# Feeding the next batch's first scan rows early, fc2 in four other banks, and identity matmuls between the tiles of layer norms

## The reference

```python
# block 0: bidirectional state-space block and gated MLP, both with adaptive layer norm
h, gate = adaln(x, c, ...)                      # LN(x) * (1 + scale) + shift
x = x + gate * (ssm(h, fwd) + flip(ssm(flip(h), bwd)))
h, gate = adaln(x, c, ...)
x = x + gate * ((silu(h @ w1) * (h @ w2)) @ w3)
# ssm: xs, z = split(h @ in_w); xs = silu(xs); dt, B, C from xs @ xproj_w
#      state[d, s] = state[d, s] * exp(dt_t * A[d, s]) + dt_t * x_t * B_t[s];  y_t = sum_s state * C_t[s]
#      y = (y + xs * Dskip) * silu(z) @ out_w          (512 channels, 64 states)
# block 1: attention with 16 heads of 16, unit-length q and k, then FFN
x1 = ln(x) * (scale1 + 1) + shift1
x = x + (softmax(unit(q) * sm @ unit(k).T) @ v @ proj_w.T + proj_b) * gamma1
x2 = ln(x) * (scale2 + 1) + shift2
x = x + (gelu(x2 @ fc1_w.T + fc1_b) @ fc2_w.T + fc2_b) * gamma2
```

## Time and profile before

| | |
|---|---|
| median of 3 runs | 3326.49 us |
| profiled execution, its own time | 3327.19 us |
| its span | 3325.4 us |
| granted TensorE clock, mean | 0.989 |
| TensorE busy | 3211.2 us (97%), weight loads 2670.8 us (80%) |
| VectorE busy | 2775.5 us (83%) |
| ScalarE busy | 2801.9 us (84%) |
| GpSimd busy | 2516.3 us (76%) |
| DMA | 187.19 MB, mean 56 GB/s |

### The profile page before, as it was taken

The page is one execution under the profiler, slowest core; times in us unless marked ns, Lnnn a source line. Parts: engine busy times, 40 slices in busy tenths (PEclk is TensorE's granted clock), DMA queues, the critical chain, the costliest instruction groups (busy, mean ns, idle before and its releaser), DMA issues.

```text
span 3325.4 us, 60434 instructions
## 1 busy us (share of the span) xinstructions
PE 3211.2 (97%) x23656; PEld 2670.8 (80%) x23656; DVE 2775.5 (83%) x2969; ACT 2801.9 (84%) x4968; POOL 2516.3 (76%) x1120
## 2 busy tenths in 40 slices
PE   8999999999899999999989999999999999999999
PEld 7989898974698988996468999899637898888854
DVE  3999999966399999996549999999555999999962
ACT  4999999955599999994569999999457999999744
POOL 3999999950299999993039999999305999999800
PEclk9999999999999999999999999999999999999999
DMA  4211212200212111120021121212002222111100
GB/s 164 71 66 52 74 52 72 65 32 1 77 55 66 67 65 63 61 69 22 1 86 58 66 69 56 71 53 71 13 1 86 64 66 65 57 58 58 39 13 7
DMA packets 57900, 187.19 MB, mean 56 GB/s; under 512 B 6664, under 2 KB 12808, under 8 KB 56848
## 3 DMA queue, kind: packets, MB, share of 16 engines
q1 hardware_dynamic: 57616, 183.33, 16.3%
HBM read 180.14 MB, written 3.16 MB: 55 GB/s over the span
## 4 chain that ended last, share of the span: by engine, by line
PE 65%; POOL 17%; ACT 8%; issue 7%; DVE 2%; DMA 1%; SPq 0%; DVEq 0%; ACTq 0%; POOLq 0%
POOL states L567 16%; PE bank L977 16%; PE bank L959 13%; PE bank L960 8%; PE bank L855 7%; ACT decay L710 4%; PE bank L1176 4%; PE bank L1049 3%; ACT inflow_tok L704 3%; PE bank L1095 2%; PE bank L1197 2%; PE bank L1276 2%; PE bank L1209 2%; DVE states L1413 1%; PE bank L1030 1%
## 5 line engine op out<-in xcount | busy, mean ns | idle before, releaser
L567 POOL TENSOR_TENSOR states<-states,c_rows 128x1024 f32<-128x1024 f32 x1020 | 2390.2, 2389 | 440.0 <-DMA c_rows<-c_spill 389.5
L1413 DVE TENSOR_TENSOR_SCAN states<-decay,bank 128x512 f32<-128x512 f32 x2048 | 2357.0, 1204 | 196.7 <-ACT decay L710 147.9
L710 ACT ACTIVATE decay<-dt,a_log 128x512 f32<-128x512 f32 x2048 | 1307.6, 714 | 0.0
L977 PE MATMUL bank<-ident,states 128*128 128x128 f32 x8192 | 1240.9, 274 | 30.2 <-POOL states L567 6.6
L959 PE MATMUL bank<-ident,inflow_tok 128*128 128x128 f32 x6144 | 1034.4, 277 | 31.7 <-DVE states L1413 16.0
L704 ACT ACTIVATE inflow_tok<-dtx_tok,b_tok 128x512 f32<-128x512 f32 x1536 | 995.9, 715 | 42.3 <-PE bank L960 39.1
L977 PEld LDWEIGHTS bank<-ident,states 128*128 128x128 f32 x8192 | 951.8, 141 | 71.3 <-POOL states L567 63.3
L959 PEld LDWEIGHTS bank<-ident,inflow_tok 128*128 128x128 f32 x6144 | 714.2, 141 | 190.9 <-issue 98.4
L960 PE MATMUL bank<-b_diag,dtx_tok 128*128 128x128 f32 x4096 | 792.4, 275 | 0.0
L960 PEld LDWEIGHTS bank<-b_diag,dtx_tok 128*128 128x128 f32 x4096 | 619.0, 191 | 0.0
L705 ACT ACTIVATE b_diag<-ident,b_tok 128x128 f32<-128x128 f32 x512 | 201.1, 393 | 0.0
(11 more groups left out here) (154 smaller groups left out, 1975.0 us busy)
## 6 DMA issues: line engine op xcount, KB each, us to landing
c_rows<-c_spill SPq DMA_DIRECT2D x256, 512.0 KB, 3.7
xproj_w<-in_xproj_w SPq DMA_DIRECT2D x32, 320.0 KB, 4.2
in_w<-in_in_w SPq DMA_DIRECT2D x16, 512.0 KB, 4.8
in_w<-in_fc_w SPq DMA_DIRECT2D x8, 512.0 KB, 5.3
xproj_w<-in_w SPq DMA_DIRECT2D x8, 512.0 KB, 5.1
xproj_w<-in_fc_w SPq DMA_DIRECT2D x4, 1024.0 KB, 4.8
x_ahead<-in_x SPq DMA_DIRECT2D x4, 512.0 KB, 5.2
y_gated<-in_mod_w SPq DMA_DIRECT2D x4, 512.0 KB, 8.3
```

The costliest lines, as they stand in the source:

```text
L567: pool.tensor_tensor(pair, pair, c_row, ALU.mult).then_inc(weighed, 1)
L710: act.activation(decay[:, r % SLOTS * KI + k, :], dt[:, d, k, :], ACT.Exp, scale=a_neg[:, d, k, s:s + 1]).then_inc(decay_ready, 1)
L977: last = pe.matmul(banks[KI + t][:, k * P:(k + 1) * P], states[:, r % SLOTS * KI + k, t * P:(t + 1) * P], ident[:], is_transpose=True, sta ...
L1413: dve.tensor_tensor_scan(states[:, slot, time], decay[:, slot, time], banks[k % INFLOW_BANKS][:, time], 0.0, ALU.mult, ALU.add).then_inc(s ...
```

## The change

- SyncE loads `c_rows` for rows 0 and 2 of the next batch right behind the wait for attention's last turned lanes, ahead of the wait for fc1; the scan's loop leaves those two out from the second batch on.
- fc2 and its residual use banks 4 to 7 (`OUT_BANK`). `add_rows` of tile t waits for gelu t + 1, which frees bank 4 + t; a new wait for all eight gelus stands ahead of fc2's products.
- ScalarE, behind the last gelu, loads the table set of Exp and feeds rows 0 and 1 of the next batch, ahead of fc2's four copies; the loop leaves those two feeds out from the second batch on.
- TensorE's wait for the copies moves from the head of a batch to the first `sum_up`, which is the first to write banks 4 to 7.
- In `ln` (layer norms 1 and 3) TensorE issues `KEEP` = 2 matmuls of the identity with 256 columns of `qkv_w` into bank 4 behind each turned tile. Nobody reads their product.

```diff
+OUT_BANK = 4
+KEEP = 2
@@ SyncE, scan loop
-                    spread_rows(b, r)
+                    if r > HALF or not b:
+                        spread_rows(b, r)
@@ SyncE, behind the scan
                     sp.wait_ge(lanes_turned, (b + 1) * NG)
+                    sp.wait_ge(c_spilled, (b * 2 + 3) * 16)
+                    spread_rows(b + 1, 0)
+                    spread_rows(b + 1, HALF)
                     sp.wait_ge(fc1_mm, (b + 1) * KF)
@@ ScalarE, copy_rows
-                    act.activation(x_of[i + 1][:, t, :], banks[t][:, 0:D], ACT.Copy).then_inc(res_copied, 1)
+                    bank = banks[OUT_BANK + t if i == 3 else t]
+                    act.activation(x_of[i + 1][:, t, :], bank[:, 0:D], ACT.Copy).then_inc(res_copied, 1)
@@ ScalarE, scan loop
-                    feed_scan(b, r)
+                    if r > 1 or not b:
+                        feed_scan(b, r)
@@ ScalarE, behind the gelus
+                if not last:
+                    act.preload_act_table_set("exp_and_others")
+                    feed_scan(b + 1, 0)
+                    feed_scan(b + 1, 1)
                 for t in range(TT):
                     act.wait_ge(res_mm, (b * RES + 3) * TT + t + 1)
                     copy_rows(b, 3, t)
@@ TensorE, ln
                 for t in range(TT):
                     ln_turn(b, i, t)
+                    for _ in range(KEEP):
+                        pe.matmul(banks[O_BANK][:, 0:D], ident[:], qkv_w[:, 0, 0:D], start=True, stop=True)
@@ TensorE, sum_up
+                    if first and not r and b and not t:
+                        pe.wait_ge(res_copied, b * 3 * TT)
@@ TensorE, batch
-                pe.wait_ge(res_copied, b * 3 * TT)
@@ TensorE, behind fc1 (add_rows and residual_tile take a bank offset, at)
                 for t in range(TT):
-                    pe.wait_ge(fc1_ready, b * KF + KH + t + 1)
-                    add_rows(t, x_att, 1)
+                    pe.wait_ge(fc1_ready, b * KF + t + 1)
+                    add_rows(t, x_att, 1, OUT_BANK)
                 pe.wait_ge(fc2_gated, b + 1)
+                pe.wait_ge(fc1_ready, (b + 1) * KF)
                 for t in range(TT):
-                    residual_tile(t, lambda c, t: gelu_h[:, c, t * P:(t + 1) * P], lambda c: fc2_w[:, c, :], KF)
+                    residual_tile(t, lambda c, t: gelu_h[:, c, t * P:(t + 1) * P], lambda c: fc2_w[:, c, :], KF, OUT_BANK)
```

More of the change, by code:

```diff
@@ L1039, in turn_high, with add_rows, residual_tile @@
                 last.then_inc(y_turned, 1)
-            def add_rows(t, x, bias=None):
-                pe.matmul(banks[t][:, 0:D], ident[:], x[:, t, :], start=True, stop=False)
+            def add_rows(t, x, bias=None, at=0):
+                pe.matmul(banks[at + t][:, 0:D], ident[:], x[:, t, :], start=True, stop=False)
                 if bias is not None:
-                    pe.matmul(banks[t][:, 0:D], ident[0:1, 0:1].to_broadcast([1, P]), bias_g[:, bias, :], start=False, stop=False)
-            def residual_tile(t, lhs, rhs, steps):
+                    pe.matmul(banks[at + t][:, 0:D], ident[0:1, 0:1].to_broadcast([1, P]), bias_g[:, bias, :], start=False, stop=False)
+            def residual_tile(t, lhs, rhs, steps, at=0):
                 for c in range(steps):
-                    last = pe.matmul(banks[t][:, 0:D], lhs(c, t), rhs(c), start=False, stop=(c == steps - 1))
+                    last = pe.matmul(banks[at + t][:, 0:D], lhs(c, t), rhs(c), start=False, stop=(c == steps - 1))
                 last.then_inc(res_mm, 1)
```

## The result

The changed kernel's median is 3297.97 us (3295.87 to 3299.85, 4 runs) beside 3327.18 us (3325.43 to 3328.09, 4 runs) for the kernel before: 29.2 us faster, ratio 0.9909, 95% interval 0.9896 to 0.9921. The forecast was 3296 us, range 3288 to 3308. In a later comparison it came to 3305.81 us (3293.57 to 3309.82, 6 runs) beside 3324.36, so 18.6 us faster, ratio 0.9936 (0.9922 to 0.995); the experiments say what the wider spread probably is.

A forecast was written before the change was run, and what follows sets the result against it. Four engines are full in the scan, so gains lie in the turns and the low clock behind layer norms: 16.2 + 14.7 = 30.9 us off 3327.19, 3296.3, less 0.7 for the median, said as 3296 us, range 3288 to 3308.

The forecast's parts named there:

- The turns: Three turns between batches, end of fc2 to row 2: 9.0 us each instead of 14.4, 14.8 and 13.95, 16.2 us gained.
- the late load sets row 2, not the late feed alone: Turn between batches: GpSimd's first product, released by the c_rows load, starts 4.3 us ahead of row 2 in every batch.
- ScalarE's cover: End of fc2: two early feeds, at most 12.0 us, fit before the third and fourth copies; uncovered, each costs 4.7 us.
- The store's landing and the wait in row 3: Scan start: out's store lands at +8.8 us, row 3's wait comes at about +9; taken at 0, bounds 0 and 1 us a turn.
- The start is kept: Scan from row 2 on: the earlier start is kept entire, the stretches of 629 us staying unchanged.
- rival B: Scan: the early start isn't kept, GpSimd runs up against its own rate; 14.7 us gained only, 3312; chance 0.06.
- The clock: Behind layer norms 1 and 3: identity matmuls keep the granted clock at 1.00 in all eight places, gaining 15.7 us.
- rival A: Behind the layer norms: the clock falls all the same; 8.3 us gained, 3318; chance 0.10.
- D: Layer norms 1 and 3: tiles turned at 1.2 GHz already, added matmuls are late; 13.6 us slower, 3340; chance 0.03.
- The cost of the added matmuls: Layer norm 3: 1.32 us don't fit into 1.23, last tile about 0.25 us late, 1.0 us in all, bounds 0 to 7.
- Rival C: Clock kept in about half the places, or falling later in attention or fc2; gain 20 to 26, 3301 to 3307; chance 0.13.
- The rule on transposes: Layer norms and scan: the skill says transposes don't engage full speed; by it the outcome lies nearer to rival A's.

The follow-up runs named there:

- e3: The changed kernel with c_rows loaded where it was before, behind the store, feeds still early: 3324.09 us, ratio 0.9991 to the kernel before.
- e4: The changed kernel with the feeds of rows 0 and 1 back behind the four copies, c_rows still loaded early: 3316.38 us, ratio 0.9967 to the kernel before.
- e6: The changed kernel with the identity matmuls in ln replaced by as many matmuls of one row: 3324.99 us, ratio 0.999 to the kernel before.
- e8: The changed kernel with fc2's identity and bias matmuls right ahead of each tile's products, not all eight ahead of all: 3293.37 us, ratio 0.99 to the kernel before.
- spread adds: The kernel of e8, measured once more beside the changed kernel on one chip: 3292.21 us, ratio 0.99 to the kernel before.
- e5: The changed kernel with the two identity matmuls behind each turned tile replaced by eight 128-column transposes: 3298.47 us, ratio 0.9923 to the kernel before.

## Why the prediction was right, step by step

**The turns: 16.2 us forecast, 16.4 measured.** Row 2 was put at 9.0 us behind the end of fc2, from batch 0's start less its late load; it came at 8.91, 8.92 and 8.92. Order and releasers are those forecast: no wait of TensorE, GpSimd's first product 3.08 us behind the last copy's start and released by VectorE's scan. The reading that "the late load sets row 2, not the late feed alone" was confirmed from both sides by e3 and e4: with the load late, row 2 comes at 14.6 to 16.0 us, with the feed late at 13.3 to 13.9. ScalarE's cover held: the third and fourth copies wait 3.07 us each for fc2, as before. The store's landing and the wait in row 3 cost nothing that shows: the stretches from row 2 on are as long as before.

**The start is kept.** The scans of batches 1 and 2 take 629.26 and 629.20 us, beside 629.32 and 629.11: rival B fell.

**The clock: 15.7 us forecast, 14.9 measured in MLP and fc1** and another 0.4 between `out_w` and the MLP. It was kept in all eight places, so rival A fell, and D with it; e6 shows that D's mechanism is real, with an addition that doesn't hold the clock.

**The cost of the added matmuls: 1.0 us forecast, none measured.** This term was mis-sized. I counted 1.32 us of TensorE's time for a tile, with the 0.44 us that a pair of transposes shows; the matmuls behind it start 0.28 us after it (845.57 against 845.29), so transposes and matmuls need about 0.28 + 0.88 = 1.16 of the 1.23 us and fit. I then pushed a lateness on from tile to tile that wasn't there; the tile's pace in layer norm 3 is set by ScalarE's copy, root and shift, and from the first normalised tile to fc1 it took 5.92 us before and 5.93 after. The last tile in the timeline after:

```profile
845.29 0.44 PE L851 MATMUL bank<-ident,x_norm 128*128 128x128 f32 x2
...
845.57 1.03 PE L861 MATMUL bank<-qkv_w,ident 128*128 128x256 f32 x4
845.77 0.81 ACT L641 ACTIVATE inflow_tok<-bank,mod 128x128 f32<-128x128 f32 x2 [0.15 <-PE bank L851]
...
846.63 1.55 PE L1291 MATMUL bank<-inflow_tok,in_w 128*128 128x512 f32 x3
```

The two matmuls (1.03 us as shown, with their tail) end as the shift does.

**What was missing.** fc2 lost 3.3 us more to the clock than before in this profile. Rival C had falls "later in attention or fc2" at 1.7 us a place. In this profile they stand where they stood, in fc2 of batches 1 and 2, and cost 1.6 us more each, inside an otherwise right forecast. The second comparison, at 3305.8 us, has the time of C's case; its one profile, of the fastest run, kept the clock in all eight places and in fc2, so the falls in its slower runs are inferred from their granted clock. I had taken the falls in fc2 as chance that stays alike. They depend on the order of the matmuls ahead of it (e8), and that order was in the profile of before.

**Luck in the number.** The mechanism of both parts is as forecast, and their two sums are off by 0.2 and 0.4 us. That the total came within 2 us is luck on top: the 1.0 us of cost that didn't come and 2.4 us of chance in attention offset the 3.3 us more that fc2 lost. With fc2's clock falling in all four batches the same kernel would take about 3305 us, 13.1 more than the 3292.2 of the spread adds (an estimate), near the upper end of the range.

**The rule on transposes.** The Trainium skill, TensorE: Matmul & The Clock Gate, Part 4 (PE-mode transpose), lets full speed not engage for transposes. e5 shows the contrary directly for float32 transposes of 128 columns: eight of them a tile held a granted 1.00 in all eight places, as the identity matmuls did. I was right to let the row decide.

## What to carry to other kernels

When a start waits for a load on one side and for a feed on the other, find the length of both chains from the same event: moving one of two nearly equal chains gives nothing, moving both gives all. Sparse work of TensorE between dense phases can be paid for at the lower clock behind it. Here work over the full height of the array that fitted into the gaps, transposes included, held the clock, while matmuls of one row didn't; eight adds, four of them of one row, were better spread among full matmuls. Don't put full-height work between small matmuls that share the array without a trial: here they lost each other's company. And where a kernel's runs spread, compare their mean granted clocks before explaining a difference of a few us.

## What the runs showed that I had not expected

- One-row matmuls keep TensorE busy and let the clock fall: as filler behind the turned tiles they left it at 0.58 to 0.76 in the following 7 us. The order of the adds ahead of fc2 alone (e8) moved the kernel by 4.6 to 13.6 us.
- Three 32-row matmuls of 512 columns take 1.13 us together, and one between two full-height transposes 1.30 us with its transpose; 21 such transposes a batch, with the low clock that came with them, cost 136 us in all (3428.3 against 3292.2).
- In the later comparison the time of the changed kernel varies over 16 us between executions (3293.57 to 3309.82), that of the version with spread adds over 2.6; in the first comparison it was 4 us (3295.87 to 3299.85).
